# Two group normalizations shared between VectorE and ScalarE, and 20 matmuls of zeros instead of 14, in a convolution and deformable-convolution kernel

## The chip, the cores and the metric

The kernel runs on one core of one Trainium2 chip. The metric is device time in microseconds (us) of one execution, from start to end of the program on that core. Three runs of the kernel before gave 338.84, 337.65 and 338.06 us, with a median of 338.06.

## The reference, cut to what matters

The input is x of 4 x 32 x 64 x 64 in fp32. Two blocks are added to it one after the other, and each reads a group norm of x with 32 groups on 32 channels, so one mean and one variance for each image and channel:

```python
x = x + L0(gn(x))
x = x + L1(gn(x))
```

- gn(v) is (v - mean) / sqrt(var + 1e-5) over the 64 x 64 pixels of one image and channel.
- L0 is two 3 x 3 convolutions (32 to 16 channels each) with a batch norm on fixed statistics; from each result a 1 x 1 convolution with two position maps gives an attention map, a 3 x 3 convolution and a sigmoid are applied to it, and the map multiplies the result.
- L1 is a deformable 3 x 3 convolution: a 3 x 3 convolution gives for each pixel and tap two offsets and a modulation, the input is sampled bilinearly there, and the samples are contracted with the weights. A batch norm over all images and a relu end it.

## The kernel before

The 128 partitions hold the 4 images times 32 channels. `x_sb` is x, 4096 elements a partition; `xpad` is its normalized form with a border of zeros, 70 rows of 66. The program is written engine by engine (`@block.sync`, `@block.gpsimd`, `@block.tensor`, `@block.scalar`, `@block.vector`); each engine's list is run in order, and the lists wait for each other on semaphores alone. There is no scheduler: what stands ahead on an engine is done first, and an engine's DMA triggers stand in the same list as its work.

**First normalization.** x arrives in five DMAs; VectorE takes statistics of eight slices of 512 (L1182), their mean and variance (L1184), and the reciprocal root (`rstd`, L1144 to L1157, the root itself by ScalarE, L922). Then VectorE alone writes `xpad` in four pieces, rows 0 to 17, 17 to 34, 34 to 49 and 49 to 64 (`NORM1`, L349; L1191 to L1194), as (x - mean) * rstd, and counts each in `norm1`.

**Turned copies.** The first convolution runs on 32 x 32 tiles of TensorE's array, 16 at a time: four chunks of 8 rows times four images, where each chunk but the first needs the images on other partitions. `turn_rows` (L377) makes these copies by DMA, from `xpad` to `hy` for the first four chunks (set 0) and to `offs` for the other four (set 1): six DMAs a set, three from SyncE's queue (L488, L489) and three from ScalarE's (L926, L927). Each waits on `norm1` for the rows that it reads.

**TensorE at the start.** It waits for piece 1, runs 14 matmuls on the zero border of `xpad` into a bank that nobody reads (`start_clock`, L634 to L642; each fp32 matmul is two instructions), and waits for piece 2 and all six DMAs of set 0 (L644). Then `conv_taps` does set 0 (144 matmuls), set 1 in two parts with `att_step(0)` between them. The rest of L0 follows: ScalarE and VectorE save the convolution's results (L939, L1238), the attention maps are made in eight chunks (`map_chunk`, L945, L1255), GpSimd adds them to x (L549), and VectorE takes the statistics of the new x (L1265).

**Second normalization.** After the eighth slice VectorE makes mean, variance and rstd again and writes `xpad` in six pieces (`NORM2`, L348; L1285 to L1287), ordered so that both halves of the image become ready together: rows 0 to 9, 30 to 39, 9 to 17, 39 to 49, 17 to 30, 49 to 64. ScalarE loads the table of Sigmoid meanwhile (L967). TensorE waits for two pieces, makes the first of eight "lead" rows (`lead(0)`, L718; the product of normalized rows with L1's weights, 16 instructions), waits for four pieces, and then alternates taps of the second convolution with leads 1 to 5 (L736 to L739). A lead needs what its predecessors left to be saved: ScalarE saves leads 0, 2, 4 and 7 (`save_lead`, L1014), VectorE leads 1, 3, 5 and 6 (L1316), and `lead(n)` waits until each engine has saved all of its leads below n:

```python
            def lead(n):

                for eng_leads, saved in ((DVE_LEADS, lead_low), (ACT_LEADS, lead_saved)):
                    done = sum(m < n for m in eng_leads)
                    if done:
                        pe.wait_ge(saved, done)
                z_rows(n, lead_at(n), 0, KW).then_inc(lead_made, 1)
```

So `lead(1)` waits for ScalarE's copy of lead 0. After the second convolution come the offsets, their way through DRAM, and from 111 to 318 us a loop over 64 steps of sampling and contraction, in which nothing is changed.

## Time and profile before

| | |
|---|---|
| median of 3 runs (337.65 to 338.84) | 338.06 us |
| the profiled execution's own time | 339.78 us |
| its span | 338.0 us |
| busy: VectorE / TensorE matmul / ScalarE / GpSimd | 276.1 / 264.2 / 233.8 / 210.1 us |
| mean granted clock of TensorE | 0.946 |

The page gives for one execution what each engine was busy with, the chain of waits that ended last, the costliest groups and the waits. A group's "mean ns" is the duration of one instruction; "idle before, releaser" is how long the engine had stood still ahead of it and what ended that. TensorE's granted clock is 1.00 (2.4 GHz) or 0.50 (1.2 GHz) in any short stretch. Most of the span is the loop; the change lies in the first 75 us.

### The profile page before, as it was taken

Reading aid. Unit: us, or ns where it says so; the run is one execution under the profiler, and the core shown is the slowest. Engines: PE = TensorE matmul, PEld = TensorE weight load, DVE = VectorE, ACT = ScalarE, POOL = GpSimd, SP = SyncE. Lnnn points to the kernel's source line nnn. Section 1 sums busy time; section 2 is a strip of 40 time slices with the busy share of each in tenths; the row PEclk is TensorE's granted clock in tenths of the full one; section 3 lists DMA queues with packets and bytes.
Section 4 is the critical chain, followed back from the end, with each engine's and each line's share of the span. In section 5 each row is a group of like instructions: output and inputs, shape, how many; then the busy total and the mean of one; then the engine's idle time right before and its main releaser. Section 6 shows DMA issues by size and latency. Waiting matters only on the chain.

```text
span 338.0 us, 16272 instructions
## 1 busy us (share of the span) xinstructions
PE 264.2 (78%) x7273; PEld 180.7 (53%) x7274; DVE 276.1 (82%) x516; ACT 233.8 (69%) x347; POOL 210.1 (62%) x162
## 2 busy tenths in 40 slices
PE   0349996989895987877898898899798999988340
PEld 0336541433434665656666666667566676767230
DVE  4942178881856999999999999999899999999676
ACT  1020175432675799988888899999899999998016
POOL 9100004700405588899889888999899998998400
PEclk9978999799996799999999999999999999999695
DMA  7891000010042121221000002100000210000006
GB/s 253 157 213 31 4 2 0 0 24 4 19 79 30 21 56 22 74 77 25 3 5 4 4 4 109 39 4 6 4 4 4 74 74 5 5 4 4 5 0 248
DMA packets 11956, 14.35 MB, mean 42 GB/s; under 512 B 4269, under 2 KB 7918, under 8 KB 11848
## 3 DMA queue, kind: packets, MB, share of 16 engines
q1 hardware_dynamic: 9852, 11.34, 11.6%
q10 hardware_dynamic: 1952, 1.34, 2.3%
q8 instruction: 58, 0.95, 1.2%
q0 software_dynamic: 80, 0.61, 0.9%
q14 instruction: 14, 0.11, 0.1%
HBM read 4.73 MB, written 2.98 MB: 23 GB/s over the span
## 4 chain that ended last, share of the span: by engine, by line
DVE 39%; PE 22%; ACT 17%; issue 7%; POOL 6%; DMA 6%; DVEq 1%; ACTq 1%; SPq 0%; POOLq 0%
DVE prod L1413 19%; DVE areg L1421 7%; ACT hx L1079 7%; PE ps L608 6%; ACT hx L972 6%; PE ps L829 5%; POOL prod L573 3%; PE ps L695 3%; PE ps L713 3%; DMA hy<-xpad 2%; DMA x_sb<-in_x 2%; DMA preg<-scratch 2%; POOL prod L577 1%; DVE x_sb L1531 1%; PE ps L681 1%
## 5 line engine op out<-in xcount | busy, mean ns | idle before, releaser
L1413 DVE TENSOR_TENSOR prod<-ps,hy 128x480 f32<-128x480 f32 (+1 forms) x256 | 138.1, 601 | 8.4 <-PE ps L829 2.3
L573 POOL TENSOR_TENSOR prod<-prod 128x832 f32<-128x832 f32 x64 | 128.8, 2012 | 17.6 <-DVE prod L1413 15.5
L829 PE MATMUL ps<-zreg,hx 64*64 64x96 f32 x4608 | 123.8, 249 | 18.1 <-DVE prod L1413 10.8
L829 PEld LDWEIGHTS ps<-zreg,hx 64*64 64x64 f32 x4608 | 109.3, 134 | 36.5 <-ACT hx L1079 24.5
L972 ACT ACTIVATE hx<-ps 128x576 f32<-128x576 f32 x129 | 77.0, 650 | 19.6 <-PE ps L713 15.3
L1079 ACT ACTIVATE hx<-hx,rbias 128x1152 f32<-128x1152 f32 x63 | 79.9, 1268 | 0.6 <-ACT hx L972 0.4
L577 POOL TENSOR_TENSOR prod<-prod 128x320 f32<-128x320 f32 x64 | 50.8, 793 | 5.0
L1421 DVE TENSOR_REDUCE areg<-prod 128x64 f32<-128x576 f32 x64 | 48.3, 755 | 2.2 <-POOL prod L577 0.2
L549 POOL TENSOR_TENSOR x_sb<-prod,x_sb 128x512 f32<-128x512 f32 x8 | 10.1, 1269 | 46.8 <-DVE prod L1255 46.8
L713 PE MATMUL ps<-wz,xpad 32*64 32x144 f32 (+1 forms) x1024 | 35.2, 324 | 2.4 <-DVE xpad L1286 1.2
L1074 ACT ACTIVATE zreg<-ps 128x576 f32<-128x576 f32 x56 | 36.9, 660 | 0.0
L681 PE MATMUL ps<-preg,sel 26*128 26x288 bf16 x256 | 27.6, 289 | 9.9 <-DMA preg<-scratch 4.0
L713 PEld LDWEIGHTS ps<-wz,xpad 32*64 32x64 f32 x1024 | 15.4, 131 | 22.9 <-issue 17.6
L608 PE MATMUL ps<-xpad,wreg 32*32 32x512 f32 x144 | 20.3, 661 | 4.4 <-DMA hy<-xpad 4.4
L695 PE MATMUL ps<-xpad,hx 32*32 32x512 f32 x576 | 20.9, 598 | 0.7 <-issue 0.4
L922 ACT ACTIVATE small<-small 128x1 f32<-128x1 f32 (+1 forms) x5 | 1.0, 203 | 28.6 <-DVE small L1149 19.0
L681 PEld LDWEIGHTS ps<-preg,sel 26*128 26x128 bf16 x256 | 8.4, 92 | 20.1 <-issue 10.1
L558 POOL CAST prod<-wreg 128x512 bf16<-128x512 f32 x4 | 3.7, 915 | 21.8 <-DVE wreg L1301 21.8
L638 PE MATMUL ps<-xpad 128*66 128x132 f32 x28 | 5.4, 381 | 14.1 <-DVE xpad L1193 14.1
L1316 DVE COPY zreg<-ps 128x1152 f32<-128x1152 f32 x4 | 5.4, 1356 | 11.9 <-PE ps L713 11.9
L1014 ACT ACTIVATE zreg<-ps 128x1152 f32<-128x1152 f32 x4 | 4.5, 1132 | 12.7 <-PE ps L713 12.7
L608 PEld LDWEIGHTS ps<-xpad,wreg 32*32 32x32 f32 x144 | 7.2, 109 | 10.7 <-issue 8.9
(154 smaller groups left out, 267.2 us busy)
## 6 DMA issues: line engine op xcount, KB each, us to landing
zreg<-zreg SPq DMA_DIRECT2D x12, 288.0 KB, 2.4
out<-x_sb SPq DMA_DIRECT2D x7, 256.0 KB, 2.1
x_sb<-in_x SPq DMA_DIRECT2D x3, 512.0 KB, 4.6
preg<-scratch SPq DMA_DIRECT2D x12, 54.0 KB
zreg<-in_pos POOLq DMA_DIRECT2D x1, 528.0 KB, 5.3
x_sb<-in_x SPq DMA_DIRECT2D x2, 256.0 KB, 7.3
scratch<-parts SPq DMA_DIRECT2D x12, 36.0 KB
scratch<-prod SPq DMA_DIRECT2D x10, 36.0 KB
```

The lines of the kernel that those rows point to most:

```text
L573: pool.tensor_tensor(slots[:, :, 0:2 * moved], slots[:, :, 0:2 * moved], slots[:, :, 2 * KEPT:6 * KK], ALU.add).then_inc(half_folded, 1)
L577: pool.tensor_tensor(slots[:, :, 0:2 * moved], slots[:, :, 0:2 * moved], slots[:, :, 2 * SUMMED:2 * KEPT], ALU.add).then_inc(folded, 1)
L608: mm = pe.matmul(ps[b * C:(b + 1) * C, at:at + BANK], w0[g, t, :], rows, start=t == 0, stop=t == KK - 1, tile_position=((b + k) % SPREAD * ...
L681: mm = pe.matmul(dist_ps(PAIR_BANKS[u])[:, h, :], sel[u * C:u * C + SELK, b, :], px[u][:, :, y // 2 * W + h * HALF:y // 2 * W + (h + 1) * ...
L695: mm = pe.matmul(ps[j * C:(j + 1) * C, at:at + BANK], woff[b * C:(b + 1) * C, t, :], xpad[b * C:(b + 1) * C, r:r + CH_ROWS, dx:dx + W], st ...
L713: mm = pe.matmul(ps[g * W:(g + 1) * W, b * BANK + at:b * BANK + at + c1 - c0], xpad[b * C:(b + 1) * C, n + g * HH, 1:1 + W], wz[b * C:(b + ...
L829: return pe.matmul(g_ps(g, h)[u * W:(u + 1) * W, k - TAPS[h][0], :, :], hx[s, (t + u) % 4, k, :], z_sb[s, b, at:at + 3, k * C:(k + 1) * C] ...
L972: act.activation(hx[:, t % 4, :, :].rearrange("p k (h x) -> p h k x", h=2), dist_ps(bank).rearrange("p h (k x) -> p h k x", k=KK), ACT.Abs)\
L1074: act.activation(z_sb[:, :, n % ZRING, at:at + ZH], zt_ps(KK * HALF, ZH), ACT.Copy)\
L1079: act.activation(dist[:, slot:slot + 2, :], dist[:, slot:slot + 2, :], ACT.Relu, bias=rbias[:, 0:1], scale=-1.0).then_inc(hx_ready, 2)
L1413: mul = vector.tensor_tensor(pv[:, n0:n1], gv, wv[:, n0:n1], ALU.mult)
L1421: vector.tensor_reduce(here, prod[:, i % 2 * 2:i % 2 * 2 + 2, :] .rearrange("p g (a n e) -> p g a e n", a=C // 2, e=2)[:, :, :, :, 0:SUMME ...
```

## The change

Both normalizations are divided between VectorE and ScalarE in pairs of pieces. VectorE keeps its form with mean and rstd. ScalarE computes Identity(x * rstd + shift), for which VectorE makes shift = -mean * rstd by one more small instruction ahead of its own pieces (`shift_ready`). `norm1` and `norm2` become two semaphores each, one for each engine, and the waits ask both for what they need (`normalized`). 20 matmuls of zeros lead the first convolution instead of 14. The second load of Sigmoid's table moves from ahead of the second normalization to behind ScalarE's copy of lead 0. ScalarE's pieces of the first normalization stand ahead of its six DMA triggers.

```diff
@@ -189,7 +189,8 @@
...
         fpad_zeroed = sem("fpad_zeroed")
-        norm1 = sem("norm1")
+        norm1 = [sem(f"norm1_{n}") for n in ("vector", "scalar")]
+        shift_ready = sem("shift_ready")
         bn0_ready = sem("bn0_ready")
@@ -202,7 +203,7 @@
...
         sig_used = sem("sig_used")
-        norm2 = sem("norm2")
+        norm2 = [sem(f"norm2_{n}") for n in ("vector", "scalar")]
         hx_ready = sem("hx_ready")
@@ -332,6 +333,9 @@
...
         REACH_TURN = 15
+        inner = xpad[:, PAD_T:PAD_T + H, 1:1 + W]
+        x3 = x_sb[:, :].rearrange("p (y x) -> p y x", y=H)
@@ -343,10 +347,11 @@
...
         ROOT_IN, ROOT_OUT, ROOT_TMP = 40, 44, 48
+        NSH, NSH2 = 52, 53
         PX_DMAS = 2 * SPREAD
         NLATE = 2 * B + 4
-        NORM2 = ((0, 9), (30, 39), (9, 17), (39, 49), (17, 30), (49, H))
-        NORM1 = (17, 34, 49, H)
+        NORM1 = ((0, 17), (17, 34)), ((34, 49), (49, H))
+        NORM2 = ((0, 9), (30, 39)), ((9, 17), (39, 49)), ((17, 30), (49, H))
         TURNS = tuple((k, b0, n) for k in range(1, SPREAD) for b0, n in ((0, SPREAD - k), (SPREAD - k, k)))
@@ -374,11 +379,18 @@
...
+        def normalized(eng, done, pieces, rows):
+            for n, sem_ in enumerate(done):
+                needed = sum(pair[n][0] < rows for pair in pieces)
+                if needed:
+                    eng.wait_ge(sem_, needed)
...
                 c = SPREAD * s + k
-                eng.wait_ge(norm1, 1 + next(i for i, end in enumerate(NORM1) if end >= min((c + 1) * CH_ROWS + 1, H)))
+                normalized(eng, norm1, NORM1, min((c + 1) * CH_ROWS + 1, H))
                 r = (b0 + k) % SPREAD
@@ -638,12 +650,12 @@
...
-            pe.wait_ge(norm1, 1)
-            start_clock(14)
-            pe.wait_ge(norm1, 2)
+            pe.wait_ge(norm1[0], 1)
+            start_clock(20)
+            normalized(pe, norm1, NORM1, SPREAD * CH_ROWS + 1)
             pe.wait_ge(turned_in[0], 16 * len(TURNS))
             conv_taps(0, range(KK)).then_inc(conv_ready, 1)
-            pe.wait_ge(norm1, 3)
+            normalized(pe, norm1, NORM1, H)
             pe.wait_ge(turned_in[1], 16 * len(TURNS))
@@ -728,16 +740,19 @@
...
-            pe.wait_ge(norm2, 2)
+            for done in norm2:
+                pe.wait_ge(done, 1)
             pe.wait_ge(wz_loaded, 16 * 4)
...
             lead(0)
-            pe.wait_ge(norm2, 4)
+            for done in norm2:
+                pe.wait_ge(done, 2)
             for n, t0, t1 in ((1, 0, 1), (2, 1, 3), (3, 3, 5), (4, 5, 7), (5, 7, 8)):
...
             conv2_taps(0, range(8, KK)).then_inc(cv_ready, 1)
-            pe.wait_ge(norm2, 6)
+            for done in norm2:
+                pe.wait_ge(done, 3)
             pe.wait_ge(lead_low, 3)
@@ -923,6 +938,11 @@
...
             root(0)
+            act.wait_ge(xpad_zeroed, 1)
+            act.wait_ge(shift_ready, 1)
+            for _, (r0, r1) in NORM1:
+                act.activation(inner[:, r0:r1, :], x3[:, r0:r1, :], ACT.Identity, bias=col(NSH), scale=col(RSTD))\
+                    .then_inc(norm1[1], 1)
             turn_rows(act, 0, TURNS[3:6])
@@ -964,7 +984,10 @@
...
             root(3)
-            act.activation(warm[:, 4:5], warm[:, 0:1], ACT.Sigmoid).then_inc(warmed, 1)
+            act.wait_ge(shift_ready, 2)
+            for _, (r0, r1) in NORM2:
+                act.activation(inner[:, r0:r1, :], x3[:, r0:r1, :], ACT.Identity, bias=col(NSH2), scale=col(RSTD2))\
+                    .then_inc(norm2[1], 1)
@@ -1016,6 +1039,8 @@
...
                 save_lead(n)
+                if n == 0:
+                    act.activation(warm[:, 4:5], warm[:, 0:1], ACT.Sigmoid).then_inc(warmed, 1)
             act.wait_ge(cv_ready, 1)
@@ -1183,15 +1208,14 @@
...
             rstd(col(RSTD), col(MV + 1), GN_EPS)
+            vector.scalar_tensor_tensor(col(NSH), col(MV), -1.0, col(RSTD), ALU.mult, ALU.mult)\
+                .then_inc(shift_ready, 1)
             vector.wait_ge(xpad_zeroed, 1)
-            inner = xpad[:, PAD_T:PAD_T + H, 1:1 + W]
-            x3 = x_sb[:, :].rearrange("p (y x) -> p y x", y=H)
-            ends = (0,) + NORM1
-            for r0, r1 in zip(ends[:-1], ends[1:]):
+            for (r0, r1), _ in NORM1:
                 vector.tensor_scalar(inner[:, r0:r1, :], x3[:, r0:r1, :], col(MV), col(RSTD),
-                                     ALU.subtract, ALU.mult).then_inc(norm1, 1)
+                                     ALU.subtract, ALU.mult).then_inc(norm1[0], 1)
@@ -1281,10 +1305,12 @@
...
-            for r0, r1 in NORM2:
+            vector.scalar_tensor_tensor(col(NSH2), col(MV2), -1.0, col(RSTD2), ALU.mult, ALU.mult)\
+                .then_inc(shift_ready, 1)
+            for (r0, r1), _ in NORM2:
                 vector.tensor_scalar(inner[:, r0:r1, :], x3[:, r0:r1, :], col(MV2),
-                                     col(RSTD2), ALU.subtract, ALU.mult).then_inc(norm2, 1)
+                                     col(RSTD2), ALU.subtract, ALU.mult).then_inc(norm2[0], 1)
```

ScalarE from its first root to its sixth copy, before:

```order
L922 ACTIVATE small<-small 128x1 [waits root_in]
L383 DMA hy<-xpad 64x660 [waits norm1]
L383 DMA hy<-xpad 32x660 [waits norm1]
L383 DMA hy<-xpad 96x660 [waits norm1]
L383 DMA offs<-xpad 64x660 [waits norm1]
```

and in the changed kernel:

```order
L937 ACTIVATE small<-small 128x1 [waits root_in]
L944 ACTIVATE xpad<-x_sb,small 128x17x64 [waits shift_ready,xpad_zeroed]
L944 ACTIVATE xpad<-x_sb,small 128x15x64
L395 DMA hy<-xpad 64x660 [waits norm1_scalar,norm1_vector]
L395 DMA hy<-xpad 32x660 [waits norm1_scalar,norm1_vector]
L395 DMA hy<-xpad 96x660 [waits norm1_scalar,norm1_vector]
L395 DMA offs<-xpad 64x660 [waits norm1_scalar,norm1_vector]
```

Two pieces of the normalization have come ahead of ScalarE's triggers. ScalarE around the second normalization, before:

```order
L965 ACT_TABLE_LOAD
L965 ACTIVATE warm<-warm 128x1
L922 ACTIVATE small<-small 128x1 [waits root_in]
L967 ACT_TABLE_LOAD
L967 ACTIVATE warm<-warm 128x1
L1014 ACTIVATE zreg<-ps 128x4x288 [waits lead_made,late_loaded,rbias_ready]
L1014 ACTIVATE zreg<-ps 128x4x288 [waits lead_made] x2
```

and in the changed kernel, where L1037 is the copy of a lead and L1043 the load of Sigmoid's table:

```order
L985 ACT_TABLE_LOAD
L985 ACTIVATE warm<-warm 128x1
L937 ACTIVATE small<-small 128x1 [waits root_in]
L989 ACTIVATE xpad<-x_sb,small 128x9x64 [waits shift_ready]
L989 ACTIVATE xpad<-x_sb,small 128x10x64
L989 ACTIVATE xpad<-x_sb,small 128x15x64
L1037 ACTIVATE zreg<-ps 128x4x288 [waits lead_made,late_loaded,rbias_ready]
L1043 ACT_TABLE_LOAD
L1043 ACTIVATE warm<-warm 128x1
L1037 ACTIVATE zreg<-ps 128x4x288 [waits lead_made] x2
```

Three pieces now stand ahead of the copy of lead 0 and the table load behind it; no further table load has appeared for Identity. TensorE's list is the same but for the count of zeros and the names that it waits for.

## Rows read from the trace of the kernel before

**Rows 1.** The chain that ended last, 10 to 50 us: start, us, what

```profile
...
12.30 0.17 DVE small L1157
...
16.72 6.99 DMA hy<-xpad
...
23.84 16.11 PE ps L608 x405
...
42.67 5.46 PE ps L608 x150
```

**Rows 2.** Timeline, 68 to 79 us: start, us, engine, line, what [idle before <-releaser]

```profile
...
68.52 1.28 ACT L967 ACT_TABLE_LOAD   x1
...
69.32 4.86 DVE L1286 TENSOR_SCALAR xpad<-x_sb,small 128x576 f32<-128x576 f32 x6
...
71.03 0.74 PE L713 MATMUL ps<-wz,xpad 32*64 32x288 f32 x16 [1.16 <-DVE xpad L1286]
71.96 1.13 ACT L1014 ACTIVATE zreg<-ps 128x1152 f32<-128x1152 f32 x1 [1.94 <-PE ps L713]
...
72.01 1.15 PE L695 MATMUL ps<-xpad,hx 32*32 32x512 f32 x32 [0.23 <-DVE xpad L1286]
...
73.14 0.74 PE L713 MATMUL ps<-wz,xpad 32*64 32x288 f32 x16
...
76.95 1.13 ACT L1014 ACTIVATE zreg<-ps 128x1152 f32<-128x1152 f32 x1 [3.86 <-PE ps L713]
```

**Rows 3.** VectorE, pieces of the first normalization: ns min/median/max, first and last start

```profile
...
L1193 DVE TENSOR_SCALAR xpad<-x_sb,small x4: 1262/1332/1407, 12.5 to 16.3; 128x1088 f32<-128x1088 f32 x2, 128x960 f32<-128x960 f32 x2
```

**Rows 4.** ScalarE, single lines, columns as in rows 3

```profile
...
L978 ACT ACTIVATE hx<-hx,rbias x3: 772/776/777, 106.6 to 310.2; 128x576 f32<-128x576 f32 x3
...
L1079 ACT ACTIVATE hx<-hx,rbias x63: 1253/1267/1326, 112.9 to 308.1; 128x1152 f32<-128x1152 f32 x63
...
L939 ACT ACTIVATE preg<-ps,small x4: 770/776/779, 35.9 to 48.8; 128x512 f32<-128x512 f32 x4
...
L987 ACT ACTIVATE hy<-offs,rbias x6: 1047/1128/1195, 94.6 to 134.4; 128x576 f32<-128x576 f32 x6
```

**Rows 5.** Timeline, 13 to 28 us, columns as in rows 2

```profile
...
13.93 2.47 SPq L383 DMA_DIRECT2D hy<-xpad  x3
...
14.05 5.43 PE L638 MATMUL ps<-xpad 128*66 128x132 f32 x28 [14.05 <-DVE xpad L1193]
15.25 2.24 ACTq L383 DMA_DIRECT2D hy<-xpad  x3
...
17.61 3.58 ACTq L383 DMA_DIRECT2D offs<-xpad  x3
...
27.36 0.35 DVE L1229 SCALAR_TENSOR_TENSOR wreg<-wreg,attu 128x128 f32<-128x128 f32 x1
```

**Rows 6.** Stretches: busy PE, PEld, DVE, ACT, POOL; PEclk, DMA share, GB/s

```profile
...
19.48:21.76 2.28, 0.00 (x0) 0.00 (x0) 0.25 (x2) 0.20 (x1) 0.00 (x0) 1.00 1.06 234
21.76:28.59 6.83, 4.75 (x84) 2.18 (x97) 4.92 (x26) 1.69 (x3) 0.00 (x0) 0.50 0.72 140
69.87:71.03 1.16, 0.00 (x0) 0.00 (x1) 1.16 (x3) 0.15 (x1) 0.00 (x0) 1.00 0.14 35
103.68:113.92 10.24, 8.40 (x111) 6.70 (x112) 7.07 (x12) 5.12 (x8) 4.32 (x6) 0.50 0.08 16
```

**Rows 7.** TensorE, matmuls of zeros, early and late, columns as in rows 3

```profile
...
L638 PE MATMUL ps<-xpad x14: 427/427/456, 14.1 to 16.9; 128*66 128x132 f32 x14
...
L638 PE MATMUL ps<-xpad x4: 276/276/277, 18.4 to 18.8; 128*66 128x132 f32 x4
```

**Rows 8.** VectorE, pieces of the second normalization: busy us, mean ns, idle before

```profile
...
L1286 DVE TENSOR_SCALAR xpad<-x_sb,small 128x576 f32<-128x576 f32 x2 | 1.7, 870 | 0.0
...
L1286 DVE TENSOR_SCALAR xpad<-x_sb,small 128x640 f32<-128x640 f32 x1 | 0.6, 610 | 0.0
L1286 DVE TENSOR_SCALAR xpad<-x_sb,small 128x512 f32<-128x512 f32 x1 | 0.5, 543 | 0.0
```


## The prediction

> **What bounds the kernel now.** I read three views, in this order: the chain of waits, the timelines of the two normalizations, and the durations of single lines. The chain for 10 to 50 us names what the start costs: behind VectorE's pieces comes the DMA of the turned rows, from 16.72 to 23.71, then TensorE's convolution without a gap until 48.13 [rows 1]. So the first stage is a normalization, a transfer and a convolution in a row. Whatever shortens one of them shifts all that follows, since the rest hangs on the convolution's results. The second normalization is the same in small: TensorE's lead 0 and its first tap both stand idle until VectorE's pieces are there [rows 2].
>
> **First normalization and its transfer.** VectorE's four pieces take 1.41 to 1.26 us each and start 1.3 apart from 12.50 [rows 3]. Now a small instruction stands ahead of them; the like of it just ahead takes 0.17 and is followed 0.20 after its start [rows 1], so VectorE starts at 12.69 and ends its first piece at 14.10. ScalarE can start at some 12.70. Its form, Identity with two per-partition operands from SBUF to SBUF, is in no row. The nearest: one operand, 576 elements 0.776 and 1152 elements 1.267, which is 0.853 ns an element; two operands, 512 elements, 0.776, against 0.721 by the first two rows, so about 0.06 to 0.08 more for the second [rows 4]. I take 0.08: 1.29 for 1088 elements, 1.18 for 960, 0.86 for 576, 0.91 for 640. The other end is the slowest row, 1.13 for 576 elements on a tile with a stride of three [rows 4], which is 0.27 more a piece of that size. ScalarE's first piece then ends at 13.99 and both are there at 14.10, where before the second piece ended at 15.2.
>
> What this moves are the triggers. SyncE's first three started at 13.93, on piece 1; they start at 14.13, 0.2 later. ScalarE's first three started at 15.25, when piece 2 was there [rows 5]; they start at 14.13 too, 1.1 earlier, if a trigger may overtake the engine's second piece, since it waits for the first ones only. If it can't, it starts at 15.1, and little is won. The last of ScalarE's three was issued at 16.72 and landed last, after 6.99 us [rows 1]. How much earlier it lands isn't shown. One end is the full 1.1, since its queue starts that much earlier. The other is 0, since the transfers' share is 1.06 before it lands [rows 6]: the link is full, and SyncE's copies share it. I take 0.9, near the full shift, because the link is full only once both queues run, and ScalarE's copies wait for their own queue's turn. So the convolution could start at 22.9 instead of 23.84.
>
> **The matmuls of zeros and the clock.** 14 of them, 28 instructions, ran from 14.05 to 19.48 [rows 5]: at first 14 starts in 2.8 us, which is 0.22 each, at the end 4 in about 0.4, some 0.12 each [rows 7]. Then TensorE stood still; the granted clock was 1.00 until 21.76 and 0.50 from there to 28.59, through the first 4.75 us of the convolution, which began at 23.84 [rows 1, 6]. In those it did at half speed what takes half the time at full: 2.4 us lost. The check: set 0 runs from 23.84 to 35.8, when ScalarE saves its first chunk [rows 4], which is 12.0 us; set 1 has the same 144 matmuls, and takes 16.11 + 5.46 - 12.0 = 9.6 [rows 1].
>
> Now 40 instructions start at 14.2. If speed rises as late as before, after some 4.2 us, 19 run at 0.22 and 21 at 0.12: they end at about 20.9. All 40 at 0.22 would end at 23.0, so in no case do they hold the convolution up by more than 0.1. Between 20.9 and 22.9 TensorE stands still for 2.0 us, instead of 4.36. Does the clock survive that? It didn't survive 2.28 us and more; it did survive 1.16 us, at 69.87 to 71.03 [rows 6]. 2.0 lies between, nearer to the fall, but a fall needs time: it came 2.28 after the last zero, and here TensorE is busy again after 2.0. So I expect set 0 at full speed from its start, 9.6 us, ending at 32.5. The profiled execution would give 2.4. Its own time lies above the median of the runs, which are 1.2 apart among themselves, so not every execution need pay as much before; I take 2.3, with 1.3 and 2.4 as its ends.
>
> Set 1's copies stay hidden behind set 0: ScalarE issued its last by 21.2 [rows 5], and with the 7 us that the slowest of set 0 took they are there by 28.2, against 32.5 now. VectorE's chain of small operations for the batch norm and the attention weights ended at 27.7 [rows 5], behind a root that ScalarE does after its six triggers, as before; it is due at 32.5 too. That cover would be gone only if the convolution ended 4 us earlier still.
>
> **Second normalization.** Before: pieces from 69.32, two ready at 70.97, lead 0 at 71.03, four ready at 71.97, the first tap 72.01 to 73.16, and lead 1 at 73.14. Lead 1 also needs ScalarE's copy of lead 0, 71.96 to 73.09: the two were just level [rows 2]. Now everything starts 0.19 later: VectorE at 69.51, ScalarE at 69.53. The first pair is ready at 70.4, so lead 0 starts 0.6 earlier, and the first tap at 71.3, 0.7 earlier. But ScalarE has three pieces ahead of its copy: 0.86 + 0.91 + 1.18, less 0.1 of overlap twice, is 2.75, until 72.28. The copy runs from 72.2 to 73.3 and lead 1 starts at 73.35. TensorE stands idle from 72.5 to 73.35 and the gain is more than spent: **0.2 us lost**. At the slow end of the price for ScalarE (0.27 more a piece, 0.8 in all) it is 1.0 lost; at the fast end, pieces that need 0.3 less, nothing. Nothing behind it is worse off: the table load behind the copy takes 1.28 and ends before 75, and ScalarE's next copy is due at 77 [rows 2]. VectorE's copy of lead 1 is due after 74, and VectorE is free at 72.
>
> Here a rule speaks against the change. VectorE did the 10-row piece in 0.61 and the 8-row piece in 0.54, but the 9-row pieces, no larger than those, in 0.87 [rows 8]: even pieces run at about half the price an element. The change gives the 10-row piece to ScalarE, for 0.91. The Trainium skill ("ScalarE: Activation LUTs", Rules for kernel authors) says to do adds and multiplies on VectorE rather than on ScalarE; and in "VectorE: DVE Perf Modes", Mode 2x_2P, that the doubled rate for one fp32 source needs an outermost dimension that is even, with which the trace agrees (0.54 against 0.87). By that rule, with the 10-row piece left on VectorE, ScalarE would end at 71.5, lead 1 would start at 72.6, and this stage would win 0.5 instead of losing 0.2: a sum 0.7 better than the one below. The sum goes by the rows.
>
> **The sum.** 0.9 + 2.3 - 0.2 = 3.0 us less. The profiled execution's own 339.78 would become 336.8. It lies 1.7 above the median of the runs, so for the median: 338.06 - 3.0 = **335.1 us**. What this measurement tells from no change is 0.3%, 1.0 us.
>
> **The rivals.**
> - The transfer lands no earlier (a full link, or triggers that don't overtake the piece). For: the share of 1.06. Against: ScalarE's queue is empty until 15.25. Then 2.3 - 0.2 = 2.1 less: 336.0. Chance 0.13.
> - The zeros don't hold the clock. For: 2.0 us of standstill is near 2.28. The convolution starts at half speed as before; 0.9 - 0.2 = 0.7 less: 337.4, not to be told from no change. Chance 0.11.
> - The second normalization costs more, because ScalarE's pieces are as slow as the strided row: 0.8 more, 335.9. Chance 0.07. Against it: rows of 64 elements that lie together.
> - Slower than before: the clock falls late, around the convolution's first matmuls, and stays low longer than the 4.75 us of busy time that it costs now. The trace has one such stretch, 10.24 us at 0.50 from 103.68, with TensorE busy for 8.4 of them [rows 6]. 10.24 at half speed cost 5.1, against 2.4: 2.7 more, less 0.7 of the other terms, is 2.0 slower: 340.1. It decides from 8.2 us of low clock within the convolution, where it costs 4.1 = 2.4 + 0.7 + 1.0. Against: the other low stretch at the start is 6.8 us, and the standstill gets shorter, not longer. Chance 0.04.
>
> **How the numbers follow.** My forecast has the remaining 0.65. Its own range takes the ends of the terms: the transfer 0 to 1.1, the clock 1.3 to 2.4, the second stage +0.3 to -1.0. All at their best give 3.8 less, 334.3; a little below that for the scatter of the runs, 333.8. The first and third rivals lie inside the range, and half of the second when it ends at 337.3. Faster by over 0.3% are the forecast and the first and third rival, 0.85, less 0.01 for bad ends together; the second rival is within 0.3% but for a part on each side; the last is slower.
>
> **What would show it.** Right: ScalarE's first trigger at about 14.1; the convolution's first matmul at 22.4 to 23.3; a granted clock of 1.00 over it, with a set 0 of 9.6 us; lead 1 released by ScalarE's copy of lead 0, about 4 us behind the start of the pieces. Wrong: a clock of 0.50 in the convolution's first microseconds, a start at 23.8 or later, or ScalarE's pieces above 1.0 us for 576 elements. A difference in the loop behind 111 us would be none of mine.

## The result and the profile after

| | before | after |
|---|---|---|
| median of 11 runs each | 338.06 us (336.51 to 340.41) | 335.25 us (333.18 to 336.92) |
| after / before | | 0.9919, 95% interval 0.9895 to 0.9942 |
| the profiled execution's own time | 339.78 us | 335.25 us |
| its span | 338.0 us | 333.5 us |
| mean granted clock | 0.946 | 0.964 |

The change wins 2.8 us; 3.0 were forecast. The profiled executions lie 4.5 apart, because the one of before lay 1.7 above its median and the one of after on it. So what the two profiles show of before is one of its longer executions. The timeline of after, 11.5 to 22 us (start, us, what, and in brackets the idle time ahead and what ended it), shows the start:

```profile
11.74 0.16 DVE L1182 SCALAR_TENSOR_TENSOR small<-small 128x1 f32<-128x1 f32 x1
11.94 0.16 DVE L1211 SCALAR_TENSOR_TENSOR small<-small 128x1 f32<-128x1 f32 x1
12.01 2.58 DVE L1217 TENSOR_SCALAR xpad<-x_sb,small 128x1088 f32<-128x1088 f32 x2
12.20 2.38 ACT L944 ACTIVATE xpad<-x_sb,small 128x1088 f32<-128x1088 f32 x2 [1.07 <-DVE small L1211]
13.44 2.78 SPq L395 DMA_DIRECT2D hy<-xpad  x3
...
13.56 7.38 PE L650 MATMUL ps<-xpad 128*66 128x132 f32 x40 [13.56 <-DVE xpad L1217]
13.58 2.92 ACTq L395 DMA_DIRECT2D hy<-xpad  x3
...
16.32 3.19 SPq L395 DMA_DIRECT2D offs<-xpad  x3
16.59 3.17 ACTq L395 DMA_DIRECT2D offs<-xpad  x3
...
21.32 0.63 PE L620 MATMUL ps<-xpad,wreg 32*32 32x512 f32 x4 [0.38 <-DMA hy<-xpad]
```

The last operation of rstd (L1182) ends at 11.90, against 12.46 before (12.30 and 0.16 in the timeline; the chain has 0.17 [rows 1]). That is 0.56 earlier, since the last part of x arrived earlier in this execution (the last four statistics start at 7.82 instead of 8.30), which is no work of the change. So all that follows is counted from that end. The convolution starts 9.42 behind it, before 11.38 behind it. ScalarE's triggers start 1.68 behind it instead of 2.79 [rows 5], though ScalarE still had its second piece to do: a trigger doesn't wait for it. The zeros now run until 20.94, and TensorE stands still for 0.38 us instead of 4.36.

ScalarE's first save of set 0, in the timeline of ScalarE of after, ends it after 10.29 us:

```profile
31.61 1.45 ACT L959 ACTIVATE preg<-ps,small 128x512 f32<-128x512 f32 x2 [8.17 <-PE ps L620]
```

The second normalization, from the timeline of after for 63 to 75 us:

```profile
64.69 0.16 DVE L1182 SCALAR_TENSOR_TENSOR small<-small 128x1 f32<-128x1 f32 x1
64.88 0.16 DVE L1308 SCALAR_TENSOR_TENSOR small<-small 128x1 f32<-128x1 f32 x1
64.96 2.37 DVE L1312 TENSOR_SCALAR xpad<-x_sb,small 128x576 f32<-128x576 f32 x3
65.08 2.76 ACT L989 ACTIVATE xpad<-x_sb,small 128x576 f32<-128x576 f32 x3 [1.01 <-DVE small L1308]
...
66.05 0.75 PE L725 MATMUL ps<-wz,xpad 32*64 32x288 f32 x16 [0.47 <-DVE xpad L1312]
...
66.91 1.15 PE L707 MATMUL ps<-xpad,hx 32*32 32x512 f32 x32
67.74 1.11 ACT L1037 ACTIVATE zreg<-ps 128x1152 f32<-128x1152 f32 x1
...
68.91 0.74 PE L725 MATMUL ps<-wz,xpad 32*64 32x288 f32 x16 [0.84 <-ACT zreg L1037]
```

Lead 0 and the first tap start 0.55 and 0.67 earlier behind rstd's end (64.85) than before, and lead 1 (68.91) 0.20 later, released by ScalarE's copy. That copy stands behind 2.76 us of pieces. The first gains are spent while TensorE waits 0.84 us.

Stage by stage in the two profiled executions:

| stretch | before | after | difference |
|---|---|---|---|
| start to the end of rstd | 12.46 | 11.90 | -0.56 |
| to the convolution's first matmul | 11.38 | 9.42 | -1.96 |
| set 0, to ScalarE's first save | 12.01 | 10.29 | -1.72 |
| to the end of the second rstd | 33.43 | 33.24 | -0.19 |
| to lead 1 | 3.86 | 4.06 | +0.20 |
| lead 1 to the first save of the second convolution | 12.99 | 12.98 | -0.01 |
| from there to the end | 251.89 | 251.60 | -0.29 |

### The profile page after: what moved, and what is told of

The parts are those of the page before. It is cut to its first block and busy times, and to the rows that moved or that the text cites. A ratio compares the mean times of both kernels' runs of the same rounds, so it can differ in the third digit from the quotient of the medians.

```text
span 333.5 us, 16311 instructions
## 1 busy us (share of the span) xinstructions
PE 264.8 (79%) x7285; PEld 182.7 (55%) x7286; DVE 271.6 (81%) x513; ACT 238.8 (72%) x352; POOL 209.8 (63%) x162
## 5 line engine op out<-in xcount | busy, mean ns | idle before, releaser
L693 PE MATMUL ps<-preg,sel 26*128 26x288 bf16 x256 | 26.9, 285 | 7.8 <-DMA preg<-scratch 4.1
L620 PE MATMUL ps<-xpad,wreg 32*32 32x512 f32 x144 | 18.5, 595 | 0.4 <-DMA hy<-xpad 0.4
L650 PE MATMUL ps<-xpad 128*66 128x132 f32 x40 | 7.4, 370 | 13.6 <-DVE xpad L1217 13.6
L650 PEld LDWEIGHTS ps<-xpad 128*66 128x66 f32 x40 | 7.2, 201 | 13.2 <-issue 13.2
L707 PEld LDWEIGHTS ps<-xpad,hx 32*32 32x32 f32 x576 | 7.4, 103 | 9.8 <-issue 8.4
```

Source lines behind the costliest of these rows:

```text
L620: mm = pe.matmul(ps[b * C:(b + 1) * C, at:at + BANK], w0[g, t, :], rows, start=t == 0, stop=t == KK - 1, tile_position=((b + k) % SPREAD * ...
L693: mm = pe.matmul(dist_ps(PAIR_BANKS[u])[:, h, :], sel[u * C:u * C + SELK, b, :], px[u][:, :, y // 2 * W + h * HALF:y // 2 * W + (h + 1) * ...
L707: mm = pe.matmul(ps[j * C:(j + 1) * C, at:at + BANK], woff[b * C:(b + 1) * C, t, :], xpad[b * C:(b + 1) * C, r:r + CH_ROWS, dx:dx + W], st ...
```

## The experiments

Each ran in five rounds beside the kernel before, with 11 or 12 runs each (6 for the third piece behind the copy and for ten rows on VectorE). Three groups of four kernels had their own runs of the kernel before, with medians of 337.06, 337.68 and 337.37; so ratios are compared, not times. "conv" is the convolution's first matmul behind the end of rstd, "stood" TensorE's standstill ahead of it (behind the last zero), "set 0" the time from the first matmul to ScalarE's first save, and "lead 1" its start behind the end of the second rstd, all in us and from one profile each. Such a profile is one execution: those of before and of even pieces on VectorE alone lay 1.7 and 1.4 us above their medians, those of ten rows on VectorE and of even pieces, shared, 1.4 and 1.7 below. The medians of before differ by up to 1.0 us between the groups, so a difference of that size between kernels of two groups is not settled.

| kernel | median us | ratio (95%) | conv | stood | set 0 | lead 1 |
|---|---|---|---|---|---|---|
| before | 338.06 | 1 | 11.38 | 4.36 | 12.01 | 3.86 |
| after | 335.25 | 0.9919 (0.9895 to 0.9942) | 9.42 | 0.38 | 10.29 | 4.06 |
| shared, 14 zeros | 335.41 | 0.9952 (0.9915 to 0.9989) | 9.04 | 2.70 | 9.87 | 4.06 |
| before, 20 zeros | 336.50 | 0.9991 (0.9954 to 1.0027) | 10.80 | 2.19 | 9.87 | 3.85 |
| only the first shared | 334.78 | 0.9927 (0.9896 to 0.9959) | 10.31 | 2.14 | 10.29 | 3.89 |
| third piece behind the copy | 334.27 | 0.9898 (0.9841 to 0.9954) | 9.86 | 1.02 | 10.03 | 3.31 |
| even pieces, VectorE alone | 336.07 | 0.9952 (0.9921 to 0.9983) | 12.10 | 4.62 | 11.11 | 3.34 |
| ten rows on VectorE | 333.10 | 0.9884 (0.9839 to 0.9930) | 9.89 | 1.29 | 10.30 | 3.31 |
| even pieces, shared | 334.12 | 0.9900 (0.9867 to 0.9934) | 9.10 | 1.18 | 10.02 | 3.35 |
| ScalarE's triggers late | 335.77 | 0.9950 (0.9915 to 0.9986) | 9.88 | 0.71 | 10.02 | 4.05 |
| set 1 behind set 0 | 335.19 | 0.9957 (0.9926 to 0.9987) | 9.37 | 2.40 | 11.61 | 4.06 |
| before, set 1 behind set 0 | 334.83 | 0.9924 (0.9894 to 0.9953) | 9.52 | 2.09 | 11.37 | 3.86 |
| even, shared, set 1 behind | 333.81 | 0.9916 (0.9881 to 0.9951) | 9.17 | 2.91 | 9.86 | 3.36 |
| after, no zeros | 336.30 | 0.9991 (0.9957 to 1.0026) | 9.50 | | 11.71 | 4.06 |

### One part of the change at a time

The changed kernel with the old number of zeros:

```diff
-            start_clock(20)
+            start_clock(14)
```

> The changed kernel with 14 matmuls of zeros instead of 20; both normalizations stay shared. Theory A (what the two traces suggest): the shared first normalization starts the convolution about 2.0 us earlier counted from the end of rstd, whatever the zeros do, and holding the clock is worth 1.7 us. With 14 zeros TensorE stands still for some 2.2 us ahead of the convolution, near the 2.28 us after which the clock fell before; if it falls, set 0 takes about 12 us instead of 10.3, and the kernel is about 1.7 us slower than the changed one and 1.1 to 1.8 faster than before. If it does not fall, this kernel is as fast as the changed one, 335.2. Rival B (the zeros matter only in that 20 of them end too late): with 14 the convolution starts up to 0.4 us earlier and the kernel is faster than the changed one.

Measured: 335.41 us, 0.9952. The convolution began 9.04 behind rstd, after 2.70 us of standstill, and yet the granted clock stayed at 1.00 and set 0 took 9.87. By the two ratios, sharing with the old number of zeros wins over half of what the change wins; the intervals overlap, and by the medians it is as fast.

The kernel before with only `start_clock(14)` changed:

```diff
-            start_clock(14)
+            start_clock(20)
```

> The kernel before with 20 matmuls of zeros instead of 14 and nothing else. Theory A: the transfer lands where it did, 11.3 us after rstd; the zeros end at about 20.9, TensorE stands still for 2.9 us, more than the 2.28 us after which the clock fell, but the fall may come only as the convolution starts or be spared: 0 to 1.7 us faster than before, set 0 in 10.3 to 12 us. Rival B (more than half of the gain is the zeros' own): 1.7 us faster or more, 336.4 or less. Rival C (the zeros are worth nothing without an earlier transfer): 338.0, set 0 12 us.

Measured: 336.50 us, 0.9991, not to be told from no change, although the profiled execution has what the zeros are for: no low clock in the convolution and a set 0 of 9.87. So the median of before doesn't pay the price of its profiled execution in full. The clock that every run lists points the same way: of 92 runs of the kernel before in the three groups, 27 have a mean granted clock of 0.947 or less, like the profiled one (0.946), and a median of 339.0 us; the other 65 have one of 336.7. With 20 zeros alone none of the 12 runs is so low, yet their mean clock is 0.954, against 0.953 for the 92 of before. The runs don't tell in which stage the low clock fell.

The first normalization shared, the second left to VectorE:

```diff
-            act.wait_ge(shift_ready, 2)
-            for _, (r0, r1) in NORM2:
-                act.activation(inner[:, r0:r1, :], x3[:, r0:r1, :], ACT.Identity, bias=col(NSH2), scale=col(RSTD2))\
-                    .then_inc(norm2[1], 1)
+            act.activation(warm[:, 4:5], warm[:, 0:1], ACT.Sigmoid).then_inc(warmed, 1)
```

> The changed kernel, but the second normalization is VectorE's alone again, with the load of Sigmoid's table where it was. Theory A (sharing the second one costs 0.2 us, because ScalarE's copy of lead 0 comes behind its three pieces): lead 1 starts 4.0 us after the end of the second rstd instead of 4.2, and the kernel is 0.2 us faster than the changed one, which runs can hardly tell. Rival B (the shared second normalization brings something that I don't see): slower than the changed kernel by 0.5 us or more.

Measured: 334.78 us, 0.9927; lead 1 at 3.89 instead of 4.06. Sharing the second normalization costs 0.17 us at lead 1 and gives nothing.

ScalarE's third piece of the second normalization moved behind its copy of lead 0:

```diff
-            for _, (r0, r1) in NORM2:
+            for _, (r0, r1) in NORM2[:2]:
...
                 if n == 0:
+                    r0, r1 = NORM2[2][1]
+                    act.activation(inner[:, r0:r1, :], x3[:, r0:r1, :], ACT.Identity, bias=col(NSH2),
+                                   scale=col(RSTD2)).then_inc(norm2[1], 1)
```

> The changed kernel, with ScalarE's third piece of the second normalization (rows 49 to 64, not needed before set 1 of the second convolution) behind its copy of lead 0. Theory A: the copy starts when lead 0 is made, 1.2 us earlier, and lead 1 follows the first tap without standstill, about 3.4 us after the end of rstd instead of 4.2: 0.8 us faster than the changed kernel, 334.4. Rival B (the next wait takes its place, ScalarE's table load and copy of lead 2 or VectorE's copies): lead 2 or 3 waits, and less than 0.3 us is left of it.

Measured: the copy starts at 2.12 instead of 2.89, lead 1 at 3.31 instead of 4.06; 334.27 us. This names the order of ScalarE's list as what spends the gain.

### The division of the pieces

VectorE alone, in pieces with an even number of rows:

```diff
-        NORM2 = ((0, 9), (30, 39), (9, 17), (39, 49), (17, 30), (49, H))
-        NORM1 = (17, 34, 49, H)
+        NORM2 = ((0, 10), (30, 40), (10, 18), (40, 50), (18, 30), (50, H))
+        NORM1 = (18, 34, 50, H)
...
+            start_clock(20)
```

> The kernel before with 20 matmuls of zeros and VectorE alone on both normalizations, but in pieces of even row counts (18, 16, 16, 14 rows; then 10, 10, 8, 10, 12, 14). Theory (in fp32, VectorE runs a piece with an even number of rows at about half the price an element): pieces of about 0.87, 0.80, 0.80 and 0.74 us instead of 1.41 to 1.26; SyncE triggers about 0.9 us and ScalarE about 1.7 us after the end of rstd, as early as with sharing; in the second normalization two pieces are ready 1.25 us and four 2.4 us after the end of rstd, and lead 1 starts at about 3.4 us, against 4.06 with sharing. The time is 334.5 us, at or below the changed kernel. Rival (the price is per element plus a fixed cost, and the 10-row piece was cheap for another reason, such as its place in the row): pieces of 1.3 us, triggers as in the kernel before, and a time of 336.5 us as with 20 zeros alone.

Its pieces, from the groups by line and shape (busy us, mean ns of one):

```profile
L1193 DVE TENSOR_SCALAR xpad<-x_sb,small 128x1024 f32<-128x1024 f32 x2 | 1.5, 806 | 0.0
L1193 DVE TENSOR_SCALAR xpad<-x_sb,small 128x1152 f32<-128x1152 f32 x1 | 0.9, 880 | 0.0
L1286 DVE TENSOR_SCALAR xpad<-x_sb,small 128x640 f32<-128x640 f32 x3 | 1.7, 610 | 0.0
L1193 DVE TENSOR_SCALAR xpad<-x_sb,small 128x896 f32<-128x896 f32 x1 | 0.7, 741 | 0.0
```

and those of after:

```profile
L1217 DVE TENSOR_SCALAR xpad<-x_sb,small 128x1088 f32<-128x1088 f32 x1 | 1.4, 1402 | 0.0
L944 ACT ACTIVATE xpad<-x_sb,small 128x1088 f32<-128x1088 f32 x1 | 1.3, 1296 | 1.1 <-DVE small L1211 1.1
L944 ACT ACTIVATE xpad<-x_sb,small 128x960 f32<-128x960 f32 x1 | 1.2, 1176 | 0.0
...
L989 ACT ACTIVATE xpad<-x_sb,small 128x640 f32<-128x640 f32 x1 | 0.9, 909 | 0.0
L989 ACT ACTIVATE xpad<-x_sb,small 128x576 f32<-128x576 f32 x1 | 0.9, 871 | 1.0 <-DVE small L1308 1.0
L1312 DVE TENSOR_SCALAR xpad<-x_sb,small 128x576 f32<-128x576 f32 x1 | 0.9, 868 | 0.0
```

18 rows take 0.88 us and 17 rows 1.40. The Trainium skill ("VectorE: DVE Perf Modes", Mode 2x_2P) gives one source the doubled rate if the outermost dimension is even, or odd and equal for source and destination. The prediction left out the second half of this condition. It doesn't apply here: the trace has the source of a 9-row piece as one run of 576 elements, and its destination as 9 rows of 64, which are not equal. The Trainium skill agrees with every shape in these kernels: 8, 10, 12, 14, 16, 18 and 20 rows run at the low price, and 9, 13, 15 and 17 don't. SyncE's first trigger came 0.94 behind rstd and ScalarE's 1.67, as expected. But the convolution did not follow: it began at 12.10, later than in any other kernel. The early trigger, which the prediction had made the cause of the gain, bought nothing in this execution; that called for the runs on the transfer below.

The changed kernel with rows 39 to 49 and 9 to 17 on VectorE:

```diff
-        NORM2 = ((0, 9), (30, 39)), ((9, 17), (39, 49)), ((17, 30), (49, H))
+        NORM2 = ((0, 9), (39, 49), (9, 17), (17, 30)), ((30, 39), (49, H))
```

> The changed kernel with the second normalization divided otherwise: VectorE does rows 0 to 9, 39 to 49, 9 to 17 and 17 to 30, ScalarE only 30 to 39 and 49 to 64. Theory (the odd division of the change cost this stage 0.7 us): the first tap still starts about 2.1 us after the end of rstd, ScalarE is done at about 2.15 and lead 1 starts at 3.3 us instead of 4.06; the time is 334.5 us, 0.7 below the changed kernel. Rival (the stage is hidden behind a later wait): lead 1 at 3.3, but the save of the second convolution's first result at 17.0 as in the changed kernel, and no gain.

The timeline of this kernel, 63.5 to 71 us:

```profile
63.92 1.95 ACT L989 ACTIVATE xpad<-x_sb,small 128x576 f32<-128x576 f32 x2 [1.01 <-DVE small L1308]
...
65.81 1.13 ACT L1037 ACTIVATE zreg<-ps 128x1152 f32<-128x1152 f32 x1
...
66.99 0.24 PEld L725 LDWEIGHTS ps<-wz,xpad 32*64 32x64 f32 x16 [1.04 <-ACT zreg L1037]
67.00 0.74 PE L725 MATMUL ps<-wz,xpad 32*64 32x288 f32 x16
```

rstd ends at 63.69, so lead 1 starts 3.31 behind it: 0.75 earlier, where the rule promised 0.7. It is kept: the first save of the second convolution comes at 16.29 instead of 17.04. 333.10 us is the lowest median of the study, though its interval overlaps that of after.

Both ideas, and fewer rows for ScalarE in the first normalization:

```diff
+        NORM1 = ((0, 20), (20, 34)), ((34, 50), (50, H))
+        NORM2 = ((0, 10), (10, 18), (40, 50), (18, 30)), ((30, 40), (50, H))
```

> Both ideas at once: VectorE takes even pieces and ScalarE fewer (first normalization: VectorE rows 0 to 20 and 34 to 50, ScalarE 20 to 34 and 50 to 64; second: VectorE 0 to 10, 10 to 18, 40 to 50, 18 to 30, ScalarE 30 to 40 and 50 to 64). Theory: SyncE and ScalarE both trigger about 1.2 us after the end of rstd, 0.35 earlier than in the changed kernel, and the convolution starts up to 0.35 earlier; lead 1 starts at 3.3 us. The time is 333.9 us, the best of all. Rival (the transfer's landing varies by more than its start is moved): the convolution starts anywhere from 9.0 to 10.3 us after rstd, and only the second stage's 0.7 us shows.

Measured: 334.12 us, 0.9900. The triggers started at 1.08 and 1.51, the convolution at 9.10, within the scatter of the others (9.04 to 10.31): the rival.

### The transfer

ScalarE's triggers of set 0 held back until both of its pieces are written:

```diff
+            act.wait_ge(norm1[1], 2)
             turn_rows(act, 0, TURNS[3:6])
```

> The changed kernel, but ScalarE triggers its three turned copies of the first set only when its second piece is written too. Theory (the earlier start of ScalarE's queue is what brings the convolution forward): the triggers start 2.8 us after the end of rstd as in the kernel before, and the convolution at about 11 us instead of 9.0 to 10.3; the time is 1 to 1.5 us above the changed kernel, 336.5 us. Rival (the link is the bound, and all six copies end when the last byte is through): with SyncE's triggers unchanged at 1.54 us the convolution starts at 10 us or earlier, and the time is 335.3 us.

Measured: the first trigger at 2.70, a full us later than in after, the convolution at 9.88. The six kernels that share the first normalization with unchanged triggers start it at 9.04 to 10.31, 9.67 on average. So the later trigger costs a few tenths at most, not 1.1. The ratio, 0.9950 against 0.9919 of after, has overlapping intervals and settles nothing.

Why so little? Three triggers of one queue take long themselves. In the changed kernel the queue of SyncE needed (ns min/median/max of one trigger):

```profile
L395 SPq DMA_DIRECT2D hy<-xpad x3: 522/652/1442, 13.4 to 15.7; - x3
```

ScalarE's third trigger, one of the two largest copies, came 4.26 behind rstd before, 3.79 in after, 4.01 here and 3.70 with even pieces on VectorE. It moved by 0.6 us at most, whatever its first did.

Set 1's copies held back until set 0 has landed, on the changed kernel with 14 zeros:

```diff
+            sync.wait_ge(turned_in[0], 16 * len(TURNS))
             turn_rows(sync, 1, TURNS[0:3])
...
-            turn_rows(act, 1, TURNS[3:6])
             root(1)
             root(2, P128, 2)
             act.activation(warm[:, 2:3], warm[:, 0:1], ACT.Sigmoid).then_inc(warmed, 1)
+            act.wait_ge(turned_in[0], 16 * len(TURNS))
+            turn_rows(act, 1, TURNS[3:6])
```

> The changed kernel with 14 matmuls of zeros and one more edit: both queues trigger the turned copies of set 1 only when all six of set 0 have landed. Theory (the copies of set 1 take a share of the link from the last of set 0: SyncE's last lands 5.5 us after its issue and the first only 4.3): the last copy of set 0 lands at about 8.2 us after the end of rstd and the convolution starts there, against 9.0 to 10.3 in the kernels with both sets in a row; set 1 is triggered from 8.2 on and lands by 16, ahead of set 0's end at 18. The time is about 1 us below the changed kernel, 334.3. Rival (each copy's time is its own, not a share): the convolution starts at 9 us or later, and nothing is won.

Measured: the convolution at 9.37, no earlier than without the edit (9.04): the rival. With the normalization shared, set 0 lands no earlier for having the link to itself.

The same edit alone on the kernel before, VectorE alone and 14 zeros:

> The kernel before with that one edit and nothing else: VectorE alone, 14 matmuls of zeros, set 1 triggered when set 0 has landed. Theory (in the kernels with VectorE alone, SyncE's copies of set 1 get ahead of ScalarE's last copy of set 0, which therefore lands 6.7 to 8.3 us after its issue instead of 4.5): the last lands at about 8.6 us after the end of rstd instead of 10.8 to 12.1, TensorE stands still for 1.6 us only and the granted clock stays at 1.00; the time is 335.5 us, as good as the changed kernel without any sharing. Rival (sharing itself brings the convolution forward, by the earlier start of the pieces): the convolution starts at 10.5 us or later and the time stays at 337.

Measured: the convolution at 9.52 instead of 11.38, and 334.83 us, 0.9924: as much as the whole change, with no normalization shared.

All six copies of set 0 count in one semaphore, and the profile gives its landings to the copies in the order of their issue. So it doesn't show how long a single copy took, but it does show the time from the last issue of the set to its last landing. In the kernel before, by the row of the copy that was issued last (247.5 KB, median us from issue to landing), that is

```profile
hy<-xpad ACTq DMA_DIRECT2D x1, 247.5 KB, 7.0
```

with even pieces on VectorE

```profile
hy<-xpad ACTq DMA_DIRECT2D x1, 247.5 KB, 8.3
```

in the changed kernel, where SyncE's third is issued last,

```profile
hy<-xpad ACTq DMA_DIRECT2D x1, 247.5 KB, 4.5
...
hy<-xpad SPq DMA_DIRECT2D x1, 165.0 KB, 5.5
```

and in the kernel before with set 1 behind set 0

```profile
hy<-xpad ACTq DMA_DIRECT2D x1, 247.5 KB, 5.4
```

With VectorE alone and both sets in a row it is 6.7 to 8.3 us in three kernels; with the first normalization shared 5.1 to 5.9 in eight; with set 1 held back 5.4 or 5.5 in three, shared or not. So the copies of set 1 delay set 0 in the kernels with VectorE alone, and little or not at all in the shared ones.

The packets of the two queues show the same. The DMA queues, from the end of rstd to the last landing of set 0 (packets, MB, share of 16 engines), q1 being SyncE's and q10 ScalarE's (its 1.01 MB in all are the six copies of ScalarE), before:

```profile
q1 hardware_dynamic: 789, 1.08, 44.7%
q10 hardware_dynamic: 368, 0.77, 34.2%
```

after:

```profile
q1 hardware_dynamic: 502, 0.85, 44.6%
q10 hardware_dynamic: 304, 0.65, 31.8%
```

and before with set 1 behind set 0:

```profile
q1 hardware_dynamic: 352, 0.54, 28.9%
q10 hardware_dynamic: 240, 0.51, 22.8%
```

Each queue has 0.51 MB of set 0, and as much of set 1 behind it. Before, SyncE's queue had moved both of its sets almost whole when ScalarE's, which started later, was through with its half of set 0. The edit holds back more than set 1: SyncE's later loads, which stand behind it, too. But these can't be the cause, since their first packets move at 23.30 in before, 0.4 us ahead of the last landing.

What decides how much set 1 delays set 0 is not settled. Behind rstd, in before SyncE's first copy of set 1 is triggered at 3.99 and ScalarE's last of set 0 at 4.26; with even pieces both at 3.70; in after set 1 starts at 4.42, 0.6 behind ScalarE's last; in the kernel with late triggers 0.5 behind. That would fit an order in which whoever comes first is served first. It does not fit the kernel before with 20 zeros, where set 1 started 0.9 behind (4.92 against 4.00) and the set still took 6.7 from its last issue.

Both lines together:

> The kernel with even pieces shared by both engines, 14 matmuls of zeros, and set 1 triggered behind set 0's landing. Theory (the two gains add): the convolution starts at about 7.8 us after the end of rstd, lead 1 at 3.3 in the second normalization, and the time is 333.2 us. Rival (they don't add, or SyncE's later loads, now 4 us later, hold something up behind the convolution): 334 us, or a stage between the convolution and the second normalization that is longer than 21.2 us.

Measured: 333.81 us, 0.9916; the convolution at 9.17, not 7.8. The two don't add: with sharing, holding set 1 back brings nothing more, as the kernel above with 9.37 showed. From its first save to the second rstd it took 33.33 us (before 33.43): SyncE's later loads held up nothing.

### The clock

The changed kernel without zeros:

```diff
-            start_clock(20)
```

> The changed kernel without any matmuls of zeros. Theory (the clock is what they buy, and half speed costs set 0 a third of its low stretch): the convolution starts at 9.0 to 10.3 us after the end of rstd as with them, at a granted clock of 0.50, and set 0 takes 12 us instead of 10.3; the time is 1.5 to 2 us above the changed kernel, 337. Rival (TensorE's clock rises by itself once the convolution runs, at little cost): set 0 takes 10.5 us and the time is 335.5.

Measured: 336.30 us, 0.9991 against 0.9919. By the ratios the 20 zeros are worth some 2.4 us with sharing (the two intervals don't touch), by the two medians, which are of different groups, only 1.05; set 0 got 1.4 longer in the profile (11.71 against 10.29). How fast the convolution went shows in a stretch of 4.75 us from its first matmul, its line alone (busy us, matmuls, granted clock, DMA share, GB/s). Nothing of this line runs ahead of the stretch, so the count is of matmuls started in it. Without zeros:

```profile
21.15:25.90 4.75, 4.75 (x97) 1.00 0.93 167
```

The kernel before:

```profile
23.84:28.59 4.75, 4.75 (x84) 0.50 0.57 113
```

After:

```profile
21.32:26.07 4.75, 4.75 (x152) 1.00 0.89 162
```

In the kernel before with set 1 behind set 0 the low clock came 0.6 us behind the first matmul. Its stretches of 1 us:

```profile
21.34:22.34 1.00, 0.99 (x32) 0.81 0.00 0
22.34:23.34 1.00, 1.00 (x33) 0.50 0.90 240
23.34:24.34 1.00, 1.00 (x33) 0.50 0.99 264
24.34:25.34 1.00, 1.00 (x33) 0.50 0.97 246
25.34:26.34 1.00, 1.00 (x49) 0.99 0.87 248
```

From the second on, these counts take in the matmuls that still run from the stretch before, 16 or 17 of them. So 33 in a stretch at 0.50 are 16 or 17 started, and 49 at 1.00 are 32: half the clock is half the rate. Before's 84 in 4.75 us are 18 a us, after's 152 are 32. In the same way set 0 grows by about half of the low stretch that falls into it. At full clock throughout it takes 9.87 at its shortest (20 zeros alone; sharing with 14 zeros). It takes 2.14 more for 4.75 us of low clock in before, 1.24 more for 2.7 with even pieces on VectorE alone, and 1.50 and 1.74 more for 3.4 and 3.2 in the two kernels with set 1 held back and a low clock.

And without zeros TensorE starts at less than two thirds of the rate of after, 97 against 152, beside a granted clock of 1.00: set 0 takes 1.84 more than 9.87. After's own 10.29 at a clock of 1.00 is 0.42 above 9.87 too; ten rows on VectorE and only the first shared have the same. The loss falls some 5 us into the convolution, and no run shows its cause.

## Why the prediction was right, and where it wasn't

The time (335.25 for 335.1), the range and the sign were right. Of the three terms one was right in cause and size; the clock was right in cause and too large in size; the transfer was too small and had the wrong cause.

- **The second normalization: right.** +0.2 was forecast, +0.20 came, by the mechanism named: ScalarE's copy of lead 0 behind its three pieces. The prices for ScalarE, 1.29, 1.18, 0.86 and 0.91, measured 1.296, 1.176, 0.871 and 0.909. Moving one piece behind the copy, or rows 39 to 49 to VectorE, removes the loss and gives 0.55 against before (lead 1 at 3.31 instead of 3.86), where 0.5 was forecast. The rival of slow pieces is out.
- **The transfer: too small, and for the wrong reason.** 0.9 with ends 0 and 1.1; in the two profiles 1.96. By the mean of six shared kernels (9.67) it is 1.7 against before's 11.38, and 1.1 against the 10.80 of the kernel before with 20 zeros, whose transfer is the same. The failed step is "ScalarE's copies wait for their own queue's turn", so that the gain would be how much earlier its queue starts. The queue starts 1.1 earlier, but its last trigger only 0.5, and holding the first back by one us hardly matters. What the kernel before loses is the delay of set 0 by set 1, which the prediction looked at only as something "hidden behind set 0". The timeline of before had it, in a line that I passed over:

```profile
16.45 3.24 SPq L383 DMA_DIRECT2D offs<-xpad  x3
```

  SyncE's copies of set 1 start ahead of 16.72, at which the last copy of set 0 is issued. The 6.99 us behind it [rows 1] are the time to the set's last landing; the prediction took them for the time of this one copy, which the profile doesn't show.
- **The clock: right in cause, too large in size.** That TensorE "did at half speed what takes half the time at full" holds: 84 matmuls instead of 152 in 4.75 us, and 2.14 us of set 0 for a forecast of 2.4. The failed step is the 9.6 us for set 0 "at full speed from its start", taken from set 1's own time. It was reached in no kernel (9.86 at best), and after lost another 0.42 at a clock of 1.00. So set 0 fell from 12.01 to 10.29, by 1.72.
- **From the profile to the median.** 2.3 of the 2.4 of one execution were carried into the median. The lower end of 1.3 was reasoned from the fact that not every execution pays as much, and that fact weighed more: 20 zeros alone kept the clock in their profile and brought 0.6 us by the medians, ratio 0.9991. How much of the 2.8 us in the median is the clock's is not shown. Sharing with 14 zeros (0.9952) both lands the transfer earlier and kept the clock in its profile. Holding set 1 back alone (0.9924) speaks for the transfer: in its profile the convolution starts 1.86 earlier, and set 0, with 3.4 us of low clock, is 0.64 shorter.
- **The sum: right in part by luck.** In the profiles the three terms are 1.96 + 1.72 - 0.20 = 3.5 instead of 0.9 + 2.3 - 0.2 = 3.0: 1.1 too little for the transfer and 0.6 too much for the clock. That the median then came to 2.8 is two errors of opposite sign and a profile of before that lay above its median.
- **The standstill.** 2.0 us were forecast between the last zero and the convolution, and 0.38 came, since the transfer landed earlier and the zeros ran until 9.04 behind rstd. They never held it up. That the clock survives 1.16 us and not 2.28 was no rule: it survived 2.70 and 2.91 with 14 zeros, and fell after 2.09, when the convolution had run for 0.6 us, and after 2.40.

The loop and all behind the second convolution changed by 0.3 us in the profiles; the prediction forecast nothing there.

## What to carry to other kernels

When a transfer's last part is slow, look at what other queues had triggered by then, not only at when its own queue began: here copies that are due much later could be held back at no cost, and two waits won as much as dividing two normalizations. When a stage is divided between engines, put what the next stage waits for ahead of what it doesn't, and leave each engine the shapes that it does cheaply. A low clock can be priced at half its busy stretch, but the price of one profiled execution is not that of the median: look first at the clocks of all runs. And read a rate from instructions that start in a stretch, not from all that overlap it.

## What the runs showed of the hardware that was not expected

- VectorE's fp32 piece of 18 rows of 64 takes 0.88 us and one of 17 rows 1.40 us.
- ScalarE's DMA triggers start while its own activation is still running: first trigger at 13.58, second piece until 12.20 + 2.38 = 14.58.
- The granted clock in the records does not tell that TensorE is slow from a cold start: without zeros 97 matmuls start in 4.75 us at 1.00, against 84 at 0.50 in before and 152 at 1.00 in after. The zeros show the same before: 0.22 us each at 1.00 and 0.12 later [rows 7].
- Half the granted clock is half the rate of these packed fp32 matmuls: 16 to 18 start in a us at 0.50, 32 at 1.00.
- Whether the clock falls around a standstill of 2.1 to 2.9 us differs between kernels, and not in the order of the standstill: it fell with 2.09 and 2.40, and not with 2.14, 2.19, 2.70 and 2.91.
- Three triggers in a row on one queue take 2.8 us in after, a single one up to 1.44 there and up to 1.97 in the kernel with only the first shared.
